# A spare product behind every product of the key loops of a graph network kernel, and seven PSUM banks instead of eight

## The chip, the cores and the metric

The kernel is one program on 1 core of a Trainium2 chip. The metric is the device time of one execution in microseconds (us). The engines are TensorE (PE, with its weight loads shown as PEld), VectorE (DVE), ScalarE (ACT), GpSimd (POOL) and SyncE (SP); 16 DMA engines move the data.

## The reference

Four graph networks run one after the other on 3125 nodes and 50000 edges, each followed by a residual sum and a layer norm. The first one is a two-layer attention network, and the change lies in its scores:

```python
for l in range(L):                                  # two layers
    xn = _layernorm(h, ln1_g[l], ln1_b[l])
    q = (xn @ wq[l] + bq[l]).reshape(n, H, DH)      # 8 heads of 32: 256 numbers a node
    k = (xn @ wk[l] + bk[l]).reshape(n, H, DH)
    v = (xn @ wv[l] + bv[l]).reshape(n, H, DH)
    scores = jnp.einsum('ehd,ehd->eh', q[dst], k[src]) * scale
    m = jax.ops.segment_max(scores, dst, num_segments=n)
    ex = jnp.exp(scores - m[dst])
    z = jax.ops.segment_sum(ex, dst, num_segments=n)
    agg = segment_sum((ex / z[dst])[:, :, None] * v[src], dst)
    ...
```

All data are float32. `dst` is sorted, so the edges of 128 successive rows have their targets in few nodes.

## The kernel before

The edges are laid out in T = 416 tiles of 128, and G = 104 groups of four tiles. For each of the two layers there is a key loop (the names are `k0` and `k1`) over the 104 groups, which makes the scores, and later a value loop (`v0`, `v1`), which sums the weighted values. The third and fourth network have edge loops of their own (`l1`, `l3`), which gather rows in the same manner. The stages follow each other: the scan after a key loop needs all its scores.

Each engine runs its own instruction stream in order, and semaphores tie them. In group i of a key loop:

- POOL issues four indirect DMAs (L944), each of which gathers 128 rows of 512 numbers (key and value of the edge's source) into a ring of five groups. Before group i it waits until group i-5 is scored, and until the value half of that slot has been written out.
- SP loads the places of the targets (LOCT), and DVE makes a one-hot matrix of them (L1466), three groups ahead. ACT copies the window of queries that belongs to each tile into QS (L2082), also three groups ahead.
- PE multiplies the one-hot by the queries (L2517), one product of 264 columns for each tile: the query of each edge, and 8 more columns. Products go round the eight PSUM banks, so that product n waits until product n-8 has been used (the semaphore `self_edge`). Each second product gives an increment of `q_edge`. A float32 product stands in the profile as two MATMUL records and two LDWEIGHTS records.
- DVE multiplies the gathered keys by the bank (L1485, one for each tile; before the first and the third of a group it waits on `q_edge`), then sums by head (L1488). This last one is what POOL waits for, as `scored`.
- ACT takes the last 8 columns of the bank after DVE's multiplication (L2093), and so frees the bank. It also issues the write of the value half to DRAM (L2090, queue q10).

The one-hot of group i+3 stands in DVE's stream behind the sum of group i, and in layer 0 a small step of another job (L1451 to L1457) stands behind that.

Of the kernel before, what the change touches and what calls it, by code (L numbers as in the profile page):

```python
# [17 lines left out]
T = 416  # L18
# [112 lines left out]
def program(nc, a, out):  # L131
    V, S, P, GP, SY = nc.vector, nc.scalar, nc.tensor, nc.gpsimd, nc.sync
# [14 lines left out]
    def view(o, *dims):  # L147
        n = int(np.prod(dims))
        ap = arena[:, o:o + n]
        if len(dims) == 1:  # L150
            return ap
        names = "abcd"[:len(dims)]
        return ap.rearrange("p (%s) -> p %s" % (" ".join(names), " ".join(names)),
                            **{names[i]: dims[i] for i in range(len(dims))})
# [10 lines left out]
    o_misc = take(4 * T + 1288)  # L165
# [17 lines left out]
    def misc(*dims, dt=F):  # L183
        ap = view(mo[0], *dims)
        mo[0] += int(np.prod(dims))
        assert mo[0] <= o_misc + 4 * T + 1288
        return ap if dt == F else ap.bitcast(dt)

    wd_i, ws_i, isrc, idst = (misc(T, dt=I) for _ in range(4))
    ident, iota, ones, tri, sh_1, sh_b = (misc(128) for _ in range(6))  # L190
    g1, a_bc, pcol = (misc(1) for _ in range(3))
    locd = misc(T)
    flag = misc(1, dt=I)
    B = view(o_B, L + 1)
    SC = view(o_S, T, 16)
# [10 lines left out]
    bank = [nc.alloc_psum_tensor(f"bank{i}", [128, 512], F) for i in range(8)]  # L206
# [241 lines left out]
    self_edge = Signal(nc, "self_edge", k0=T, k1=T)  # L448
# [561 lines left out]
    def vector_engine():  # L1010
# [448 lines left out]
        for l in LAYERS:  # L1459
            name = f"k{l}"  # L1460
# [18 lines left out]
            for i in range(G):  # L1479
                rows = KV[:, i % 5, :, 0:256]  # L1480
                V.wait_ge(*gathered(name, i))
                for k in range(4):
                    if k % 2 == 0:
                        V.wait_ge(*q_edge(name, 2 * i + k // 2 + 1))
                    V.tensor_tensor(rows[:, k, :], rows[:, k, :], bank[(4 * i + k) % 8][:, 0:256],  # L1485
                                    ALU.mult).then_inc(qk.sem, 1)
                V.wait_ge(*qk(name, 4 * i + 4))
                V.tensor_reduce(SC[:, 4 * i:4 * i + 4, 0:8], rows.rearrange("p k (h d) -> p k h d", d=32), AX,  # L1488
                                ALU.add).then_inc(scored.sem, 1)
                if i + 3 < G:  # L1490
                    k_onehot(i + 3)
                if l == 0:
                    source_place(i)
                    if i == 12:
                        d.mark(V.tensor_reduce(anyf, B[:, 0:L], AX, ALU.min))
                    elif i == 14:
                        V.wait_ge(*back_in("flags", 1))
                        d.settle()
                        V.tensor_reduce(anyb, B[:, 1:L + 1], AX, ALU.min).then_inc(small_in.sem, 1)

            wn, name = f"w{l}", f"v{l}"
# [27 lines left out]
            for it in range(G + 2):  # L1529
# [4 lines left out]
                if it < G:  # L1534
                    V.wait_ge(*group_in(f"v{l}", it))
                    rows = VR[:, it % VRING].rearrange("p k (h d) -> p k h d", d=32)
                    if it < 2:
                        d.mark(V.memset(WV4[it][:, :, 272:273], 1.0))
                for half in range(2):
                    if it >= 2:  # L1540
                        add_v(name, it - 2, half, v_banks(l, it - 2))
                    if it < G:
                        k = 2 * half
# [198 lines left out]
        for it in range(G + 4):  # L1742
            i = it - 1
            if 0 <= i < G:
                rows = view(o_ring, 6, 4, 72)[:, i % 6]
# [9 lines left out]
            i = it - 2  # L1755
            if 0 <= i < G:
                rows = view(o_ring, 6, 4, 72)[:, i % 6]
# [12 lines left out]
            i = it - 4  # L1770
# [228 lines left out]
    def scalar_engine():  # L1999
# [70 lines left out]
        for l in LAYERS:  # L2070
            if l == 1:
                S.wait_ge(*w_landed(W_LOADS["layer1"]))
            name = f"k{l}"
# [12 lines left out]
            for i in range(G):  # L2086
                if i + 3 < G:
                    stage(i + 3)
                S.wait_ge(*gathered(name, i))
                S.dma_start(VE[i], KV[:, i % 5, :, 256:512]).then_inc(kept[i % 5].sem, 16)  # L2090
                for k in range(4):
                    S.wait_ge(*qk(name, 4 * i + k + 1))
                    S.activation(SC[:, 4 * i + k, 8:16], bank[(4 * i + k) % 8][:, 256:264],  # L2093
                                 ACT.Identity, bias=FL[:, 4 * i + k:4 * i + k + 1]).then_inc(self_edge.sem, 1)
            for k in range(5):
                S.wait_ge(*kept[k]((l + 1) * len(range(k, G, 5))))
# [9 lines left out]
            name = f"v{l}"  # L2106
# [124 lines left out]
        for it in range(G + 4):  # L2231
            if it < 4 * W:
                copy_blocks(2 * it)
            i = it - 1
# [6 lines left out]
            i = it - 2  # L2241
# [91 lines left out]
    def tensor_engine():  # L2333
# [168 lines left out]
        for l in LAYERS:  # L2502
            if l == 1:
                P.wait_ge(*w_landed(W_LOADS["layer1"]))
            name = f"k{l}"
            P.wait_ge(*self_made(f"qkv{l}", W))
            P.wait_ge(*taken(f"mix{l - 1}", 5 * W) if l else taken("qkv0", 3 * W))
            for i in range(G):
                if l == 0 and i == 0:
                    P.wait_ge(*back_in("flags", 1))  # L2510
                P.wait_ge(*onehot(name, i + 1))
                P.wait_ge(*placed(name, i + 1))
                for k in range(4):
                    b_ = bank[(4 * i + k) % 8]
                    if 4 * i + k >= 8:
                        P.wait_ge(*self_edge(name, 4 * i + k - 7))
                    mm = P.matmul(b_[:, 0:264], OHQ[:, i % 3, k * 128:(k + 1) * 128], QS[:, i % 4, k, :],  # L2517
                                  start=True, stop=True)
                    if k % 2:
                        mm.then_inc(q_edge.sem, 1)  # L2520
            if l == 0:
                P.wait_ge(*scan_in("w0", 1))
                answer()
                P.transpose(bank[6][0:1, 0:128], anyf, ident)
                P.transpose(bank[6][0:1, 128:256], anyb, ident).then_inc(small_out.sem, 1)
# [326 lines left out]
```

## Time and profile before

| | |
|---|---|
| Median of 3 runs | 5205.84 us (5201.02 to 5213.5) |
| The profiled execution: its time | 5207.07 us |
| The profiled execution: its span | 5205.9 us |
| Mean granted TensorE clock | 0.835 of full speed |
| PE busy | 3587.0 us, 69% of the span |
| DVE busy | 2874.2 us, 55% |
| ACT busy | 1846.5 us, 35% |
| POOL busy | 3690.2 us, 71% |

The span runs from the first to the last instruction. Busy time is the union of an engine's instructions; time in which an engine waits on a semaphore isn't busy. In the tables by stretch, PEclk is the granted clock of TensorE, where 1.00 is 2.4 GHz and 0.50 is 1.2 GHz. A row of the timeline ends with the time that the engine sat idle before it, and what ended the idle time as far as the profile can infer it; "remote" and "issue" mean that it can't name an instruction.

### The profile page before, as it was taken

The page shows a single profiled execution, that of the slowest core. Times are in us where ns is not written, and L with a number is a line of the kernel's source. Part 1 is how long each engine was busy: PE and PEld are TensorE (multiplying, and loading weights), DVE is VectorE, ACT ScalarE, POOL GpSimd, SP SyncE. Part 2 cuts the span into 40 slices and gives each one's busy share as a digit, 9 for nine tenths or more (in the row PEclk, how much of TensorE's full clock was granted, in tenths as well). Part 3 has the DMA queues.
Part 4 walks back from the last instruction along what each step waited for, and adds up shares of the span by engine and source line. Part 5 has one row for each costly group of instructions (what it writes and reads, how often), then busy time and mean ns, then how long its engine had stood idle before and what let it go on. Part 6 is the DMA issues. An engine that isn't in the chain of part 4 may idle for free.

```text
span 5205.9 us, 59946 instructions
## 1 busy us (share of the span) xinstructions
PE 3587.0 (69%) x15291; PEld 2665.8 (51%) x15291; DVE 2874.2 (55%) x6726; ACT 1846.5 (35%) x5462; POOL 3690.2 (71%) x3085
## 2 busy tenths in 40 slices
PE   4554444466897444439979946666589999688886
PEld 3433323344575232326646634444368887577776
DVE  6465556888543454568884336677752224244445
ACT  1143333566333343337753311111120100256565
POOL 4466666888888666678888876666787887866664
PEclk9866676899898667669999868777799999789988
DMA  7688888565324888866653245566569899556565
GB/s 262 195 278 285 270 288 245 130 159 130 55 25 110 273 272 284 276 183 177 169 138 34 14 91 171 172 173 175 100 153 269 240 267 253 152 174 175 174 175 141
DMA packets 710880, 951.03 MB, mean 183 GB/s; under 512 B 273285, under 2 KB 482228, under 8 KB 710408
## 3 DMA queue, kind: packets, MB, share of 16 engines
q0 software_dynamic: 298192, 385.84, 31.0%
q1 hardware_dynamic: 204146, 388.26, 23.7%
q10 hardware_dynamic: 208198, 173.03, 10.1%
q8 instruction: 131, 2.15, 0.2%
q14 instruction: 213, 1.74, 0.1%
HBM read 727.03 MB, written 219.80 MB: 182 GB/s over the span
## 4 chain that ended last, share of the span: by engine, by line
PE 28%; issue 24%; DVE 15%; POOL 15%; another core or an unknown queue 9%; DMA 6%; ACT 2%; DVEq 1%; ACTq 1%; POOLq 0%; SPq 0%
PE bank L2677 10%; POOL ATT L981 7%; POOL sc L967 7%; PE bank L2802 6%; PE bank L2799 4%; DVE arena L1485 3%; DMA sc<-arena 2%; PE bank L2382 2%; PE bank L2517 2%; DMA ATT<-arena 2%; DVE arena L1395 2%; DVE arena L1765 2%; PE bank L2658 1%; DVE arena L1466 1%
## 5 line engine op out<-in xcount | busy, mean ns | idle before, releaser
L944 POOL DMA_INDIRECT arena<-KVT,arena x832 | 800.7, 962 | 484.5 <-issue 268.4
L2517 PE MATMUL bank<-arena 128*128 128x264 f32 x1664 | 599.0, 514 | 674.5 <-issue 332.2
L2517 PEld LDWEIGHTS bank<-arena 128*128 128x128 f32 x1664 | 390.9, 251 | 881.9 <-issue 588.3
L997 POOL DMA_INDIRECT arena<-ATTR,arena x416 | 666.8, 1603 | 152.2 <-issue 152.2
L967 POOL DMA_INDIRECT sc<-arena x391 | 641.4, 1640 | 130.4 <-issue 110.9
L981 POOL DMA_INDIRECT ATT<-arena x391 | 643.1, 1645 | 125.6 <-issue 114.0
L1485 DVE TENSOR_TENSOR arena<-arena,bank 128x256 f32<-128x256 f32 x832 | 297.4, 412 | 579.8 <-remote 426.8
L944 POOL DMA_INDIRECT arena<-X1T,arena x416 | 413.2, 993 | 245.9 <-issue 134.9
L944 POOL DMA_INDIRECT arena<-YT,arena x416 | 407.4, 979 | 218.5 <-issue 106.5
L2474 PE MATMUL bank<-arena 128*128 128x273 f32 x1664 | 455.0, 411 | 141.3 <-DVE arena L1544 91.7
L2290 ACT ACTIVATE arena<-arena 128x128 f32<-128x128 f32 x1248 | 374.8, 387 | 275.9 <-DVE arena L1371 160.8
L2658 PE MATMUL bank<-arena 128*128 128x261 f32 x832 | 318.5, 534 | 194.3 <-DVE arena L1395 156.7
L2802 PE MATMUL bank<-arena 128*128 128x128 f32 x2496 | 397.2, 293 | 79.7 <-issue 78.9
L2802 PEld LDWEIGHTS bank<-arena 128*128 128x128 f32 x2496 | 382.1, 207 | 125.6 <-issue 99.5
L2093 ACT ACTIVATE arena<-bank,arena 128x8 f32<-128x8 f32 x832 | 208.6, 265 | 651.7 <-issue 452.2
L2474 PEld LDWEIGHTS bank<-arena 128*128 128x128 f32 x1664 | 294.4, 191 | 261.8 <-DVE arena L1544 128.0
L1383 DVE TENSOR_TENSOR arena<-arena,bank 128x273 f32 x832 | 363.5, 437 | 114.9 <-DVE arena L1383 69.4
L1944 DVE TENSOR_TENSOR arena<-arena,bank 128x256 f32 x416 | 173.3, 417 | 356.6 <-remote 245.0
L2382 PE MATMUL bank<-arena 128*128 128x256 f32 (+1 forms) x1200 | 312.2, 402 | 55.9 <-ACT arena L2037 22.5
L2658 PEld LDWEIGHTS bank<-arena 128*128 128x128 f32 x832 | 186.1, 252 | 296.8 <-DVE arena L1765 159.5
L2082 ACT ACTIVATE arena<-arena 128x264 f32 x832 | 283.5, 411 | 151.3 <-issue 118.1
L2114 ACT ACTIVATE arena<-arena 128x128 f32<-128x128 f32 x832 | 265.7, 390 | 193.1 <-PE bank L2474 153.9
(334 smaller groups left out, 6434.5 us busy)
## 6 DMA issues: line engine op xcount, KB each, us to landing
VE<-arena ACTq DMA_DIRECT2D x208, 512.0 KB
arena<-VE SPq DMA_DIRECT2D x208, 512.0 KB
left<-ATT SPq DMA_DIRECT2D x250, 320.0 KB
left<-AM SPq DMA_DIRECT2D x250, 320.0 KB
ATT<-arena POOLq DMA_DIRECT2D x25, 1600.0 KB, 6.5
arena<-LOCT SPq DMA_DIRECT2D x156, 256.0 KB
arena<-ATT SPq DMA_DIRECT2D x75, 384.0 KB
AM<-arena ACTq DMA_DIRECT2D x75, 384.0 KB
```

What stands on the lines that cost most here:

```text
L944: GP.indirect_dma_start(out=ring[:, i % n, k, :], out_offset=None, in_=table, in_offset=bass.IndirectOffsetOnAxis(ap=idx[:, 4 * i + k:4 * ...
L967: GP.indirect_dma_start(out=tg3[k], out_offset=bass.IndirectOffsetOnAxis(ap=poss[:, c:c + 1], axis=0), in_=code[:, c:c + 2], in_offset=Non ...
L981: GP.indirect_dma_start(out=ATT, out_offset=bass.IndirectOffsetOnAxis(ap=PLACE[:, c:c + 1], axis=0), in_=ones[:, 0:1], in_offset=None, bou ...
L997: GP.indirect_dma_start(out=PA[:, c, 2:6], out_offset=None, in_=ATTR, in_offset=bass.IndirectOffsetOnAxis(ap=PA[:, c, 0:1].bitcast(I), axi ...
L1485: V.tensor_tensor(rows[:, k, :], rows[:, k, :], bank[(4 * i + k) % 8][:, 0:256], ALU.mult).then_inc(qk.sem, 1)
L2290: ins = S.activation(SCALED[i % 4][:, k, c, :], OH3[:, i % 3, 128 * k:128 * (k + 1)], ACT.Copy, scale=PA[:, 4 * i + k, 2 + c:3 + c])
L2382: mm = P.matmul(b_[:, 0:cols], xt[:, k * 128:(k + 1) * 128], wt[:, k, :], start=(k == 0), stop=(k == 1))
L2474: mm = P.matmul(bank[banks[k]][:, 0:r.shape[-1]], oh[:, k * 128:(k + 1) * 128], r, start=True, stop=True)
L2517: mm = P.matmul(b_[:, 0:264], OHQ[:, i % 3, k * 128:(k + 1) * 128], QS[:, i % 4, k, :], start=True, stop=True)
L2658: mm = P.matmul(bank[4 + k][:, 0:261], OH8[:, i % 8, k * 128:(k + 1) * 128], WV4[i % 2][:, k, 0:261], start=True, stop=True)
L2677: mm = P.matmul(sum_bank(n // W, j)[:, :], left[:, 128 * j:128 * (j + 1)], right[:, u, :], start=(u == 0), stop=(u == W - 1))
L2802: mm = P.matmul(s4[:, 0:m + 1:m], by[:, m, :], r8[:, m + 3:8:4 - m], start=False, stop=(m == 3), skip_group_check=True)
```

## The change

In both key loops each product of L2517 is followed by a second matmul on PE: the 128x128 identity times 384 columns of constants, into bank 7. Nothing waits for it, nothing reads it, and it gives no increment. Since bank 7 is taken, the real products go round seven banks: product n now waits for the use of product n-7. DVE and ACT read the bank by the same rule.

```diff
@@ program
     ident, iota, ones, tri, sh_1, sh_b = (misc(128) for _ in range(6))
     g1, a_bc, pcol = (misc(1) for _ in range(3))
+    SPARE_COLS = view(o_misc + 4 * T, 384)
@@ vector_engine
-                    V.tensor_tensor(rows[:, k, :], rows[:, k, :], bank[(4 * i + k) % 8][:, 0:256],
+                    V.tensor_tensor(rows[:, k, :], rows[:, k, :], bank[(4 * i + k) % 7][:, 0:256],
                                     ALU.mult).then_inc(qk.sem, 1)
@@ scalar_engine
-                    S.activation(SC[:, 4 * i + k, 8:16], bank[(4 * i + k) % 8][:, 256:264],
+                    S.activation(SC[:, 4 * i + k, 8:16], bank[(4 * i + k) % 7][:, 256:264],
@@ tensor_engine
                 for k in range(4):
-                    b_ = bank[(4 * i + k) % 8]
-                    if 4 * i + k >= 8:
-                        P.wait_ge(*self_edge(name, 4 * i + k - 7))
+                    b_ = bank[(4 * i + k) % 7]
+                    if 4 * i + k >= 7:
+                        P.wait_ge(*self_edge(name, 4 * i + k - 6))
                     mm = P.matmul(b_[:, 0:264], OHQ[:, i % 3, k * 128:(k + 1) * 128], QS[:, i % 4, k, :],
                                   start=True, stop=True)
                     if k % 2:
                         mm.then_inc(q_edge.sem, 1)
+                    P.matmul(bank[7][:, 0:384], ident, SPARE_COLS, start=True, stop=True)
```

The view of 384 columns begins where `ident` begins: it holds `ident`, `iota` and `ones`.

## Rows read from the trace of the kernel before

**Rows 1.** POOL's gathers, one row of the line for each loop: count, duration, starts.
```profile
L944 POOL DMA_INDIRECT arena<-KVT,arena x416: 940/946/2557, 256.5 to 884.9; - x139
...
L944 POOL DMA_INDIRECT arena<-KVT,arena x416: 940/946/1188, 1657.9 to 2287.3; - x139
...
L944 POOL DMA_INDIRECT arena<-YT,arena x416: 940/946/1471, 4535.4 to 5160.1; - x139
```

**Rows 2.** Windows of k0, k1, l1 and l3: us, busy, PEclk, DMA share, GB/s.
```profile
core 0: us, PE busy (x) PEld busy (x) DVE busy (x) ACT busy (x) POOL busy (x), PEclk, DMA share, GB/s
275.00:899.00 624.00, 300.99 (x831) 197.90 (x832) 371.90 (x727) 242.95 (x822) 393.98 (x405) 0.69 0.84 278
1665.00:2295.00 630.00, 290.50 (x816) 187.93 (x816) 309.62 (x616) 232.84 (x812) 394.75 (x415) 0.69 0.83 275
3057.00:3757.00 700.00, 447.04 (x1873) 308.98 (x1873) 462.04 (x1351) 117.92 (x409) 447.43 (x439) 0.77 0.58 158
4535.00:5163.00 628.00, 524.75 (x3229) 474.96 (x3230) 276.80 (x605) 369.42 (x1231) 407.56 (x417) 0.90 0.61 174
```

**Rows 3.** One turn of POOL's cycle in k0, windows of its gathers alone.
```profile
535.98:566.82 30.84, 23.47 (x24) 0.72 0.93 317
566.82:572.47 5.65, 0.00 (x1) 0.50 0.26 82
```

**Rows 4.** POOL's waits in the stretch of k0: us in total, times, longest.
```profile
POOL arena L944 <- issue: 127.6, 379, 2.5
POOL arena L944 <- DVE arena L1488: 87.5, 18, 6.6
POOL arena L944 <- DMA VE<-arena: 4.7, 6, 3.2
```

**Rows 5.** Timeline of PE in that turn: start, us, what, count [idle before].
```profile
534.48 2.13 PE L2517 MATMUL bank<-arena 128*128 128x264 f32 x4 [0.58 <-ACT arena L2093]
537.74 6.14 PE L2517 MATMUL bank<-arena 128*128 128x264 f32 x16 [1.13 <-ACT arena L2093]
544.75 2.02 PE L2517 MATMUL bank<-arena 128*128 128x264 f32 x8 [0.86 <-ACT arena L2082]
548.31 2.02 PE L2517 MATMUL bank<-arena 128*128 128x264 f32 x8 [1.54 <-issue]
551.82 1.13 PE L2517 MATMUL bank<-arena 128*128 128x264 f32 x4 [1.49 <-issue]
556.17 2.13 PE L2517 MATMUL bank<-arena 128*128 128x264 f32 x4 [3.22 <-issue]
566.91 2.10 PE L2517 MATMUL bank<-arena 128*128 128x264 f32 x4 [8.61 <-issue]
```

**Rows 6.** Timeline of DVE in that turn, and one wait of the next.
```profile
547.13 1.40 DVE L1485 TENSOR_TENSOR arena<-arena,bank 128x256 f32<-128x256 f32 x4
...
550.98 0.73 DVE L1485 TENSOR_TENSOR arena<-arena,bank 128x256 f32<-128x256 f32 x2
555.39 0.75 DVE L1485 TENSOR_TENSOR arena<-arena,bank 128x256 f32<-128x256 f32 x2 [3.69 <-remote]
...
566.04 0.75 DVE L1485 TENSOR_TENSOR arena<-arena,bank 128x256 f32<-128x256 f32 x2 [7.71 <-remote]
570.19 0.75 DVE L1485 TENSOR_TENSOR arena<-arena,bank 128x256 f32<-128x256 f32 x2 [3.40 <-PE bank L2517]
570.98 1.22 DVE L1488 TENSOR_REDUCE arena<-arena 128x32 f32<-128x1024 f32 x1
...
591.12 0.75 DVE L1485 TENSOR_TENSOR arena<-arena,bank 128x256 f32<-128x256 f32 x2 [3.19 <-issue]
```

**Rows 7.** Records since the loop began: first PE (L2517), then DVE (L1485).
```profile
270.00:554.00 284.00, 142.73 (x388) 93.89 (x388) 0.68 0.84 284
...
270.00:554.00 284.00, 66.44 (x186) 0.68 0.84 284
```

**Rows 8.** Windows inside that turn, all engines.
```profile
533.50:542.40 8.90, 7.18 (x16) 4.68 (x16) 8.59 (x17) 5.40 (x18) 4.89 (x6) 0.50 0.56 165
542.60:551.70 9.10, 5.33 (x22) 3.64 (x20) 9.03 (x19) 6.06 (x21) 6.92 (x7) 1.00 1.02 346
...
569.60:572.40 2.80, 1.43 (x3) 1.18 (x4) 2.17 (x4) 1.37 (x5) 0.00 (x0) 0.50 0.00 0
```

**Rows 9.** PE in l3, timeline of one stretch.
```profile
4742.95 0.83 PE L2802 MATMUL bank<-arena 128*128 128x128 f32 x6
4743.62 0.60 PE L2799 MATMUL bank<-arena 128*128 128x256 f32 x2
4744.05 0.83 PE L2802 MATMUL bank<-arena 128*128 128x128 f32 x6
```

**Rows 10.** POOL's waits in l3.
```profile
POOL arena L944 <- issue: 106.5, 347, 0.5
POOL arena L944 <- remote: 83.9, 49, 3.8
POOL arena L944 <- PE bank L2802: 28.1, 20, 1.8
```

## The prediction

> **What bounds the kernel now.** The page gives no engine above 71% of the span, so the share of busy time decides nothing; I read the change's own loops. First the gathers by line: POOL issues 416 of them from 256.5 to 884.9 in k0 and from 1657.9 to 2287.3 in k1 [rows 1]. That is 628.4/415 = 1.514 us each, 6.06 us a group, and 6.07 in k1. Then the windows: in both key loops PE is busy for less than half the time at a mean clock of 0.69, DVE for 60% and 49%, and the DMA engines for 0.84 and 0.83 [rows 2]. Nothing is full. So I looked at one turn of POOL's pattern. It issues 24 gathers, six groups, in 30.84 us, 5.14 a group, and then stands still for 5.65 us [rows 3]; 36.49/6 = 6.08 us a group, which is the rate of the whole loop. Its waits for DVE's head sum are 87.5 us in 18 such places [rows 4].
>
> What holds DVE at the end of a turn? It waits 3.69 us before 555.39, 7.71 before 566.04 and 3.40 before 570.19 [rows 6]. The counts say what these are: by 554.0 PE has 388 records since the loop began, which are 194 products, and DVE has started 186 multiplications [rows 7]. Products 187 and 188, for which DVE waits until 555.39, stand in PE's row that ends at 546.77 (544.75 + 2.02) [rows 5]. The wait is the one on `q_edge` (the wait on the gather stands before the first tile of the group, and this is its third). So an increment of PE comes 8.6 us behind the recorded end of its product. Three more come at once later: DVE goes on at 570.19, when the DMA share has just gone to 0.00 [rows 8], and not again held until the next turn. I call this a hold. What makes it the trace doesn't show. It does show that PE works behind the held product (548.31 and 551.82 [rows 5]) without freeing it; that it sets in while the clock is 1.00 and the DMA share 1.02 [rows 8]; and when: POOL starts its run at 535.98 and DVE's first held step ends 19.4 us later; it starts again at 572.47 and that step ends at 591.12, 18.7 us later [rows 3, 6]. It looks tied to POOL's run, not to what PE does.
>
> The key loops are thus bound by a chain: hold, head sum, five slots of the ring, POOL. PE has slack, and between holds DVE sets the pace: 547.13 to 550.98 is 3.85 us for a group [rows 6].
>
> **The change part by part.** *Spare products:* 832 of them. Four real products take 2.02 us at clock 1.00, the last one's own duration included [rows 5]; by starts I use the edge loop l3, which has the same operation and nothing between: 256 columns take 4744.05 - 4743.62 = 0.43 us, three times 128 columns 0.67 [rows 9]. That is 0.0017 us a column: 264 columns take 0.445 us and 384 take 0.65. At clock 0.50 four records of a row (two products) take 2.13 us against 1.13 [rows 5], so everything doubles. A product with its spare is 1.09 us at 1.00, 2.18 at 0.50; a group is 4.4 or 8.7 us, against 1.8 or 3.6 before. The weight loads of 0.19 us lie beside the columns. *Work added:* 832 x 0.65 = 541 us at full clock. If all of it lay on the path, the time would be 5747; but 4.4 us is under POOL's 5.14 a group, so none of it must. That cover is gone while the clock is 0.50 (8.7 over 5.14).
>
> *Seven banks:* PE can run 7 products ahead of ACT and not 8. In the row at 551.82 it is at its limit [rows 5], so it stops one product sooner during a hold. It then has nothing to deliver that isn't held, and at the end of a hold the increments that DVE needs are of products long done. I cost this at 0 to 0.1 us a turn; with 35 turns at most 4 us. *Addressing on DVE and ACT:* nothing. *Queues:* in PE's stream the spare stands between the first product of a pair and the second, which alone increments: each increment is 0.65 us later at full clock, 1.3 at half. Behind it wait DVE's multiplication, ACT's L2093 and, through the head sum, POOL. SP and POOL issue nothing new.
>
> *What this does to a turn.* From 534.48 to 546.77 PE makes 14 products (4, 16 and 8 records [rows 5]). With spares, and the clock at 0.50 until 542.5 as now [rows 8], it makes (542.5 - 534.5)/2.18 = 3.7, then 4.3/1.09 = 3.9: 7.6 products, 6.4 fewer. If the denser work raises the clock 3 us sooner, it is 9.0, 5 fewer. That is 1.25 to 1.6 groups fewer before the hold sets in, if it sets in at the same time after POOL's start. DVE has then scored fewer groups, POOL's run ends as many groups sooner (ring of five), and the stop of 5.65 us stays. A turn of n groups takes 5.14n + 5.65: n = 6 gives 6.08 a group, 4.75 gives 6.33, 4.4 gives 6.42. Over 208 groups that is +52 to +71 us; I take +60. The bounds: PE's lead of 8 products at the start of a turn hides all, 0; a whole two groups are lost, 6.55, +98.
>
> *Sum:* the profiled span is 5205.9 us with 1.2 us around it, 5207.1, and the median of the runs is 5205.8, so one stands for the other. 5206 + 60 = **5266 us**.
>
> At one place a page of the Trainium skill bears on the step of the hold. Perfetto Trace Analysis, section Tensor Engine Instruction, says that the profiler's end of a matmul is an estimate and that its semaphore goes out once PSUM has acknowledged all bytes. The 8.6 us above is such a gap, if the page is right; by it a spare product, which writes 384 more columns, could be one more thing to acknowledge and lengthen a hold, and no row before has one.
>
> **The rivals.**
>
> *No change.* PE's 4.4 us stay under POOL's 5.14, and the lead of 8 products covers the cold start. For it: l3 is as dense as the changed loops would be (PE busy 524.75 of 628, clock 0.90 [rows 2]) and POOL gets 624.7/415 = 1.505 us a gather, 6.02 a group [rows 1], the same. Against: l3 has a lower DMA load, 174 against 278 GB/s [rows 2], and its stops are short, at most 3.8 us [rows 10] against 6.6. Time: 5206, within 10 us.
>
> *Faster: the holds shrink.* In l3 with its dense PE the longest wait of POOL is 3.8 us, and POOL's waits but for the regular 0.3 us are 112 us, against 92 in k0 [rows 4, 10]. If PE that is never idle, or stays at 1.00, gets its increments out sooner, stops go. With no stop at all POOL's 5.14 would hold: 208 x 0.94 = 196 us, 5010. If half of the stops goes: 5108. The point from which this decides is a stop under 5.65 us with six groups still in a turn. Against it: PE's work behind the held product frees nothing now [rows 5], and l3's total is no smaller.
>
> *Slower by much: the half clock.* If the clock stays at its mean of 0.69, a product with spare takes 1.09/0.69 = 1.58 us, 37.9 us for the 24 of a turn, and PE idles some 10 us of it in the holds as now (8.61 and 3.22 [rows 5]): 48/6 = 8.0 us a group, +400 us, 5606. For it: the idle stretches before 556.17 and 566.91 are what the clock falls in now, 0.50 by 569.6 [rows 8]. Against: l3 has 0.90, l1 0.77 with PE busy 64% [rows 2]; the changed loops need PE for 4.4 of some 6.3 us, 70%. The Trainium skill, TensorE: Matmul & The Clock Gate, section What's actually happening, says that the throttled state is the default and activity releases it, which the rows of l3 bear out.
>
> *The change doesn't do its work* can't be: the spare is an instruction like the others and depends on nothing.
>
> **How the numbers follow.** Fewer groups a turn, +20 to +110: 0.42. No change: 0.15. Holds shrink: 0.28, half of it below 5110. Half clock, wholly or for a good part: 0.09. Longer holds as by the page, +110 to +200: 0.06. What a measurement here can tell from no change is 0.2%, 10 us. Slower: 0.42 + 0.09 + 0.06 = 0.57; same 0.15; faster 0.28. The range of 8 in 10 reaches from 5115 (the holds half gone) to 5345 (+98 and some of the longer holds); the likeliest case alone has 5226 to 5316.
>
> **What would show it.** In the profile after: a row of PE with 832 records a loop for the spare, starts 1.09 us apart at 1.00; PE busy in the key loops from 49% to some 75%, clock above 0.8; POOL's turns of 4 or 5 groups with stops near 5.65 us, and its starts in k0 655 rather than 628 us apart. Stops of 2 to 3 us with six groups would show the faster rival; PE in one unbroken row at 0.50 that ends last before DVE, the half clock. I am wrong if the hold isn't tied to POOL's run but to PE's idleness or to the number of products behind it: then the sign turns.

## The result, and the profile after

The changed kernel takes 5252.19 us (median of 4 runs, 5246.43 to 5258.68) against 5203.43 us for the kernel before (4 runs, 5196.83 to 5213.5). The ratio is 1.0095, interval 1.0081 to 1.011: 49 us slower, where 60 were forecast. The profiled execution took 5248.5 us, its span is 5247.4, which is 41.5 above that of before, and the mean granted clock rose from 0.835 to 0.885. Lines of the changed kernel stand one further down: L945 is L944 of before, L1486, L1489, L2094 and L2518 are L1485, L1488, L2093 and L2517, and the spare is L2522.

The first view is that of [rows 1], the gathers of each loop; the three answers and the row of `l1` are put together here.

```profile
L945 POOL DMA_INDIRECT arena<-KVT,arena x416: 940/946/2552, 260.7 to 909.0; - x139
...
L945 POOL DMA_INDIRECT arena<-KVT,arena x416: 940/946/1207, 1677.9 to 2325.6; - x139
...
L945 POOL DMA_INDIRECT arena<-YT,arena x416: 940/946/1439, 4577.6 to 5199.0; - x139
```

From the first gather to the last, `k0` went from 628.4 to 648.3 us and `k1` from 629.4 to 647.7: 6.25 and 6.24 us a group against 6.06 and 6.07. These 38.2 us are nearly all of the 41.5. `l3`, which the change doesn't touch, is the same but for 3.3 us (621.4 against 624.7), and the first gather starts 4.2 us later.

The windows of the same loops, as in [rows 2], say what filled them:

```profile
core 0: us, PE busy (x) PEld busy (x) DVE busy (x) ACT busy (x) POOL busy (x), PEclk, DMA share, GB/s
275.00:919.00 644.00, 505.95 (x1653) 333.63 (x1654) 374.12 (x729) 248.39 (x826) 400.06 (x408) 0.90 0.84 271
1686.00:2335.00 649.00, 504.84 (x1630) 333.30 (x1629) 307.85 (x610) 232.46 (x807) 394.26 (x414) 0.88 0.82 268
4577.00:5205.00 628.00, 524.68 (x3233) 475.51 (x3234) 276.69 (x605) 370.29 (x1234) 408.30 (x417) 0.90 0.63 175
```

PE is busy for 78 to 79% of both key loops at a clock of 0.90 and 0.88, where it was busy for 46 to 48% at 0.69, and is still not full.

POOL's waits in `k0` answer to [rows 4]:

```profile
POOL arena L945 <- issue: 138.6, 384, 2.9
POOL arena L945 <- DVE arena L1489: 99.6, 26, 5.8
...
POOL arena L945 <- DMA VE<-arena: 1.5, 5, 0.3
```

There are 26 waits for the head sum instead of 18, and they are shorter: 3.8 us on the mean against 4.9. POOL's timeline shows the new turn, of which the first and the last gathers stand here (the column in brackets is POOL's idle time before the row):

```profile
496.18 0.94 POOL L945 DMA_INDIRECT arena<-KVT,arena  x1 [4.54 <-DVE arena L1489]
497.43 0.95 POOL L945 DMA_INDIRECT arena<-KVT,arena  x1 [0.30 <-issue]
...
515.24 0.95 POOL L945 DMA_INDIRECT arena<-KVT,arena  x1 [0.30 <-issue]
521.28 0.94 POOL L945 DMA_INDIRECT arena<-KVT,arena  x1 [5.09 <-DVE arena L1489]
...
546.48 0.94 POOL L945 DMA_INDIRECT arena<-KVT,arena  x1 [4.34 <-DVE arena L1489]
```

From 496.18 to 515.24 POOL starts 16 gathers, four groups where [rows 3] had six, and stands still for 5.09 us. The turn is 521.28 - 496.18 = 25.10 us, 6.28 a group.

Now the chain inside that turn. First DVE, as in [rows 6]:

```profile
500.35 1.39 DVE L1486 TENSOR_TENSOR arena<-arena,bank 128x256 f32<-128x256 f32 x4
...
503.83 1.40 DVE L1486 TENSOR_TENSOR arena<-arena,bank 128x256 f32<-128x256 f32 x4
505.27 1.22 DVE L1489 TENSOR_REDUCE arena<-arena 128x32 f32<-128x1024 f32 x1
...
509.19 0.75 DVE L1486 TENSOR_TENSOR arena<-arena,bank 128x256 f32<-128x256 f32 x2 [1.76 <-PE bank L2518]
519.00 0.75 DVE L1486 TENSOR_TENSOR arena<-arena,bank 128x256 f32<-128x256 f32 x2 [9.06 <-remote]
519.79 1.22 DVE L1489 TENSOR_REDUCE arena<-arena 128x32 f32<-128x1024 f32 x1
```

Then PE, as in [rows 5], where x2 is one product or one spare:

```profile
504.15 0.61 PE L2518 MATMUL bank<-arena 128*128 128x264 f32 x2
504.60 0.81 PE L2522 MATMUL bank<-arena 128*128 128x384 f32 x2
505.24 0.61 PE L2518 MATMUL bank<-arena 128*128 128x264 f32 x2
505.69 0.81 PE L2522 MATMUL bank<-arena 128*128 128x384 f32 x2
506.33 0.61 PE L2518 MATMUL bank<-arena 128*128 128x264 f32 x2
...
511.78 0.61 PE L2518 MATMUL bank<-arena 128*128 128x264 f32 x2
512.23 0.81 PE L2522 MATMUL bank<-arena 128*128 128x384 f32 x2
519.77 1.25 PE L2518 MATMUL bank<-arena 128*128 128x264 f32 x2 [6.74 <-ACT arena L2094]
```

And the counts since the loop began, as in [rows 7], of PE's L2518 and then of DVE's L1486:

```profile
270.00:519.50 249.50, 103.23 (x306) 0.90 0.82 269
...
270.00:518.90 248.90, 52.62 (x146) 0.90 0.82 269
```

PE has made 153 products and DVE has started 146 multiplications. The product at 511.78 is thus number 153, and they follow each other by 1.09 us, as forecast. Number 154 needs the bank of number 147: PE stands at the limit of seven banks. Number 148, for which DVE waits until 519.00, starts at 506.33 and ends at 506.94: its increment arrives 12.1 us later, when POOL has been still since 516.19 (515.24 + 0.95). Number 146 ends at 504.76, and DVE, idle for 1.76 us, goes on only at 509.19, 4.4 us behind it. That step is the first of its group and so waits for the gathered rows too, but it isn't these that it waits for: ACT, which waits for the same rows before it issues the write of the value half, issues it at 507.19.

So this hold begins with a product that ends 8.6 us after POOL's start. In the turn of before the first held product ended at 546.77, 10.8 us after POOL's start at 535.98 [rows 3, 5], and two held steps still came through while POOL was issuing, at 555.39 and 566.04 [rows 6]; here it is one, at 509.19. The increments of before weren't the less late: products 189 to 192 stand in the row that ends at 550.33 (548.31 + 2.02) [rows 5], and DVE got the last of them at 570.19, 19.9 us later, when POOL stood still there too. Note also what DVE does until 507: its steps at 500.35 and 503.83 come 3.5 us apart with no idle time before them. PE had products ready. Two turns don't make a rule, though; all turns of the two loops stand below, with the sizes of the spare.

### The profile page after: what moved, and what is told of

Its sections match the earlier page's. It is cut to its first block, busy times and chain, and to the rows that moved or that the text cites. A ratio compares the mean times of both kernels' runs of the same rounds, so it can differ in the third digit from the quotient of the medians.

```text
span 5247.4 us, 63274 instructions
## 1 busy us (share of the span) xinstructions
PE 4020.3 (77%) x16955; PEld 2955.4 (56%) x16955; DVE 2879.2 (55%) x6726; ACT 1852.7 (35%) x5462; POOL 3691.2 (70%) x3085
## 4 chain that ended last, share of the span: by engine, by line
POOL 25%; issue 24%; PE 20%; DVE 11%; another core or an unknown queue 9%; DMA 6%; SPq 3%; DVEq 1%; ACT 1%; POOLq 0%; ACTq 0%
POOL arena L998 12%; POOL sc L968 7%; POOL ATT L982 6%; PE bank L2804 6%; PE bank L2522 5%; PE bank L2518 4%; PE bank L2801 4%; DMA ATT<-arena 3%; DMA sc<-arena 3%; SPq L646 2%; DVE arena L1486 2%; DVE arena L1396 2%; DVE arena L1766 2%; DVE arena L1372 1%
## 5 line engine op out<-in xcount | busy, mean ns | idle before, releaser
L945 POOL DMA_INDIRECT arena<-KVT,arena x832 | 803.8, 966 | 525.5 <-issue 272.3
L2518 PE MATMUL bank<-arena 128*128 128x264 f32 x1664 | 565.5, 424 | 293.5 <-ACT arena L2094 177.9
L2522 PE MATMUL bank<-arena 128*128 128x384 f32 x1664 | 724.4, 519 | 0.0
L2518 PEld LDWEIGHTS bank<-arena 128*128 128x128 f32 x1664 | 334.1, 207 | 574.6 <-ACT arena L2094 227.5
L1486 DVE TENSOR_TENSOR arena<-arena,bank 128x256 f32<-128x256 f32 x832 | 300.3, 414 | 610.7 <-remote 443.5
L945 POOL DMA_INDIRECT arena<-X1T,arena x416 | 412.4, 991 | 247.2 <-issue 136.3
L945 POOL DMA_INDIRECT arena<-YT,arena x416 | 408.0, 981 | 214.6 <-issue 107.1
L2291 ACT ACTIVATE arena<-arena 128x128 f32<-128x128 f32 x1248 | 374.8, 387 | 282.6 <-issue 144.7
L2094 ACT ACTIVATE arena<-bank,arena 128x8 f32<-128x8 f32 x832 | 212.7, 265 | 692.4 <-issue 425.5
L2804 PEld LDWEIGHTS bank<-arena 128*128 128x128 f32 x2496 | 382.3, 206 | 125.1 <-issue 98.5
L2475 PEld LDWEIGHTS bank<-arena 128*128 128x128 f32 x1664 | 295.3, 192 | 263.7 <-DVE arena L1545 136.1
L2522 PEld LDWEIGHTS bank<-arena 128*128 128x128 f32 x1664 | 342.8, 206 | 67.9
L2660 PEld LDWEIGHTS bank<-arena 128*128 128x128 f32 x832 | 188.9, 255 | 283.7 <-DVE arena L1766 138.7
```

The lines of the kernel that those rows point to most:

```text
L945: GP.indirect_dma_start(out=ring[:, i % n, k, :], out_offset=None, in_=table, in_offset=bass.IndirectOffsetOnAxis(ap=idx[:, 4 * i + k:4 * ...
L2291: ins = S.activation(SCALED[i % 4][:, k, c, :], OH3[:, i % 3, 128 * k:128 * (k + 1)], ACT.Copy, scale=PA[:, 4 * i + k, 2 + c:3 + c])
L2475: mm = P.matmul(bank[banks[k]][:, 0:r.shape[-1]], oh[:, k * 128:(k + 1) * 128], r, start=True, stop=True)
L2522: P.matmul(bank[7][:, 0:384], ident, SPARE_COLS, start=True, stop=True)
L2660: mm = P.matmul(bank[4 + k][:, 0:261], OH8[:, i % 8, k * 128:(k + 1) * 128], WV4[i % 2][:, k, 0:261], start=True, stop=True)
L2804: mm = P.matmul(s4[:, 0:m + 1:m], by[:, m, :], r8[:, m + 3:8:4 - m], start=False, stop=(m == 3), skip_group_check=True)
```

## The experiments

The theories at the start were these. *Rate*: PE's time for the spares cuts the number of products made before the hold (the prediction). *Lost bank*: seven banks instead of eight. *Count*: not the time but the number of instructions that PE issues while POOL gathers brings the hold on. *Position*: the increment of each pair stands behind the spare of its first product. In the expectations these are A (*rate*), B (*lost bank*), D and F (*count*) and E (*position*); G, which comes up later, has any matmul behind a product cost the whole, however many records it has. The diffs are against the changed kernel, but for those of `one_pass` and `ring_of_four`, which are against the kernel before.

### The bank alone

`seven_banks` has no spares and keeps the rule of seven.

```diff
-                    P.matmul(bank[7][:, 0:384], ident, SPARE_COLS, start=True, stop=True)
```

> The changed kernel without its spare products: only the seven banks are left. Theory A (PE with its spares makes fewer products before the hold sets in, so POOL's turn has four or five groups instead of six): no change to the kernel before, ratio 0.999 to 1.001, POOL's turns still of 24 gathers, 628 us from first to last gather in k0. Rival B (the lost bank does it: PE stops one product sooner and the hold bites sooner): ratio 1.007 to 1.010, turns of 16 to 20 gathers.

5211.01 us against 5208.06 on the same chip, ratio 1.0004 (0.9993 to 1.0015). *Lost bank* falls: alone it costs nothing that can be told from nothing, as the prediction had it (4 us at most). No run has the spares with eight banks.

### The size of the spare

`spare64` writes 64 columns, `spare512` writes 512.

```diff
-                    P.matmul(bank[7][:, 0:384], ident, SPARE_COLS, start=True, stop=True)
+                    P.matmul(bank[7][:, 0:64], ident, SPARE_COLS[:, 0:64], start=True, stop=True)
```

> The changed kernel with spares of 64 columns instead of 384: a product with its spare takes about 0.56 us at full clock and 1.1 at half. Theory A: in the 12.3 us between POOL's start and the hold PE makes (8/1.1) + (4.3/0.56) = 15 products, no fewer than the 14 of before, so nothing is lost: ratio 0.998 to 1.002, turns of 24 gathers. Rival D (it is the number of instructions or of PSUM writes behind the products that lengthens the hold, not PE's time): ratio 1.006 to 1.010 as in the changed kernel.

> The changed kernel with spares of 512 columns: a product with its spare takes 1.31 us at full clock, 5.25 us a group, above the 5.14 that POOL needs. Theory A: (8/2.6) + (4.3/1.31) = 6.3 products instead of 14 before the hold, 1.9 groups fewer: 6.5 to 6.7 us a group, +90 to +130 us on the kernel before, ratio 1.017 to 1.025. If instead the lead of eight products hides PE's time until it passes POOL's rate: some 1.012.

| spare | us | ratio (interval) | k0, first to last gather |
|---|---|---|---|
| none | 5211.01 | 1.0004 (0.9993 to 1.0015) | 632.5 |
| 64 columns | 5253.84 | 1.0091 (1.0074 to 1.0108) | 649.2 |
| 384 columns | 5252.19 | 1.0095 (1.0081 to 1.011) | 648.3 |
| 512 columns | 5257.04 | 1.01 (1.008 to 1.0119) | 651.7 |

The kernel before took 5208.06 us beside the first, second and fourth, and 5203.43 beside the third. The window 275 to 875 us of the three kernels, in the order none, 64, 512:

```profile
275.00:875.00 600.00, 283.96 (x799) 183.66 (x797) 349.74 (x681) 235.68 (x790) 389.13 (x396) 0.69 0.84 281
```

```profile
275.00:875.00 600.00, 365.56 (x1557) 308.72 (x1558) 345.75 (x673) 235.04 (x779) 373.40 (x384) 0.72 0.82 272
```

```profile
275.00:875.00 600.00, 527.28 (x1525) 297.20 (x1526) 342.48 (x666) 233.23 (x770) 369.20 (x382) 0.96 0.82 271
```

PE's busy time goes from 284 to 366 to 527 us and its clock from 0.69 to 0.72 to 0.96. POOL's gathers in the window, the count beside its busy time, go from 396 to 384 to 382. The whole price comes with the first 64 columns. This is a clear fall of *rate*, and it also clears the clock: 0.72 and 0.96 cost the same. Two of POOL's stops in `spare64` (starts with the idle time before them):

```profile
532.12 0.94 POOL L945 DMA_INDIRECT arena<-KVT,arena  x1 [3.90 <-DVE arena L1489]
557.36 0.94 POOL L945 DMA_INDIRECT arena<-KVT,arena  x1 [4.84 <-DVE arena L1489]
```

What the sizes share shows when all turns of a loop are read in the traces. A turn is here what POOL issues between two stops of over 1.5 us, from the sixth group on. A product counts as held when DVE stands idle for over 0.8 us and starts its multiplication over 1.5 us after the recorded end, with the gathered rows there for over 1 us by ACT's issue of the value half. Each entry has `k0` and `k1`; the last two columns are medians over the 14 to 27 turns that have a held product.

| kernel | turns | groups a turn | products from POOL's start to the first held one | its end, us after POOL's start |
|---|---|---|---|---|
| before | 22, 24 | 4.5, 4.1 | 13, 13 | 10.8, 9.0 |
| no spares, seven banks | 22, 25 | 4.5, 4.0 | 14, 12 | 12.8, 8.5 |
| 64 columns | 28, 30 | 3.5, 3.3 | 8, 7 | 7.0, 5.7 |
| 384 columns | 30, 30 | 3.3, 3.3 | 8, 8 | 8.7, 8.1 |
| 512 columns | 30, 31 | 3.3, 3.2 | 8, 7 | 10.2, 8.5 |

Without spares the hold begins with the 12th to 14th product, with them with the 7th or 8th, whatever the columns. The time at which it begins grows with the columns, and with 512 it is nearly that of the kernel before (10.2 and 8.5 us against 10.8 and 9.0), at the full price; so it isn't an earlier hold that costs, but one after fewer products. In MATMUL records it is some 24 to 28 without spares and 28 to 32 with them, which fits *count* best.

### The place of the spare

`spares_after_pair` puts both spares of a pair behind its increment.

```diff
                     if k % 2:
                         mm.then_inc(q_edge.sem, 1)
-                    P.matmul(bank[7][:, 0:384], ident, SPARE_COLS, start=True, stop=True)
+                        for _ in range(2):
+                            P.matmul(bank[7][:, 0:384], ident, SPARE_COLS, start=True, stop=True)
```

> The same 832 spares of 384 columns, but both of a pair stand behind the pair's second product, so that the increment of a pair isn't 0.65 us (1.3 at half clock) later for the spare in its middle. PE's work is the same. Theory A (PE's rate decides): as the changed kernel, ratio 1.008 to 1.011. Rival E (the lateness of each increment decides): half of the loss goes, ratio 1.003 to 1.006.

5254.04 us against 5208.06, ratio 1.0091 (1.0075 to 1.0108); `k0` takes 647.8 us from its first gather to its last. The same as the changed kernel: *position* falls. Its turns have 3.2 groups, and the first held product is the 8th. Of the four theories *count* is left, and G beside it.

### Fewer and other instructions, on chips that have no holds

The next four were to bend the count: spares in bfloat16 (one MATMUL record each), one spare of 64 columns a group, the real products in one pass without spares, and a ring of four slots instead of five without spares. `one_pass` makes the one-hot and the queries float32r, so the queries are rounded to that type before the product.

```diff
+    IDENT_BF = ident.bitcast(BF)[:, 0:128]
+    COLS_BF = ident.bitcast(BF)[:, 128:192]
...
+                    P.matmul(bank[7][:, 0:64], IDENT_BF, COLS_BF, start=True, stop=True)
```

> The changed kernel with spares of 64 columns in bfloat16 (on the bits of the identity, whatever they say), which are one MATMUL record and one LDWEIGHTS record each and not two: 12 MATMULs a group instead of 16. The spares of 64 columns cost as much as those of 512, so theory A (PE's time) has fallen. Theory F (the number of MATMUL instructions that PE issues while POOL gathers brings the hold on): the loss goes with the records, half of it, ratio 1.003 to 1.006, turns of five groups. Rival G (any instruction behind the product, once it is there, costs the whole): 1.008 to 1.010.

```diff
-                    P.matmul(bank[7][:, 0:384], ident, SPARE_COLS, start=True, stop=True)
+                P.matmul(bank[7][:, 0:64], ident, SPARE_COLS[:, 0:64], start=True, stop=True)
```

> The changed kernel with one spare of 64 columns behind the fourth product of a group only, float32: 10 MATMULs a group. Theory F: a quarter of the loss, ratio 1.001 to 1.004. Rival G: 1.008 or so, if what matters is that a matmul stands behind an increment and before PE's next wait.

```diff
-    OHQ = view(o_acc, 3, 512)
+    OHQ = exact("ohq", o_acc, 3, 512)
-    QS = view(o_acc + 1536, 4, 4, 264)
+    QS = exact("qs", o_acc + 1536, 4, 1056).rearrange("p a (b c) -> p a b c", b=4)
```

> The kernel before, with its real products of the key loops in float32r (the one-hot and the copied queries are written as float32r), without spares, eight banks. The queries are rounded to that type. The hop products of the same kernel, in float32r, have one MATMUL record each, so a group would have 4 records and not 8. Theory F: longer turns, some seven or eight groups, 5.9 to 6.0 us a group, ratio 0.992 to 0.998. Rival G, and theory A with PE's slack: no change, 0.999 to 1.001.

```diff
+                if i >= 4:
+                    GP.wait_ge(*scored(k_, i - 3))
...
-                    GP.wait_ge(*scored(k_, i - 4))
```

> The kernel before, where POOL waits until group i-4 is scored, not i-5, as if the ring of gathered rows had four slots; nothing else. If the hold is tied to what happens during POOL's run and POOL's stop follows when the ring is full, a turn has five groups: (5.14 x 5 + 5.65)/5 = 6.27 us a group, +43 us, ratio 1.006 to 1.010. If a shorter run has a shorter stop, as the changed kernel has (4.3 against 5 us by the median), less: 1.002 to 1.006. If the stops come from the DMA load, which a smaller ring smooths: no change or faster.

They ran on another chip, on which the kernel before took 4811.96 us:

| | us | ratio (interval) |
|---|---|---|
| spare_bf16 | 4813.46 | 0.9998 (0.9985 to 1.0011) |
| spare64_per_group | 4816.67 | 1.0007 (0.9994 to 1.002) |
| one_pass | 4814.43 | 0.9999 (0.9985 to 1.0012) |
| ring_of_four | 4817.73 | 1.0007 (0.9994 to 1.002) |

Nothing here moves the time, and some 395 us are gone from all, the kernel before included. The four can't decide between the theories, since what they disagree about isn't there. So the changed kernel itself was run again on one more chip, beside the spare in bfloat16:

> The changed kernel itself once more, since the last four kernels ran on a chip on which the kernel before takes 4812 us instead of 5208, POOL hardly ever stops in the key loops (5.15 to 5.19 us a group) and no variant differs. If this run falls on such a chip: with no hold there is nothing for the spares to bring forward, PE's 4.4 us a group stay under POOL's 5.15, ratio 0.998 to 1.002. On a chip with holds: 1.008 to 1.011 as recorded.

> The spares of 64 columns in bfloat16, one MATMUL record each, 12 a group, again. On a chip with holds, theory F (the number of MATMUL instructions brings the hold on) expects half of the loss, 1.003 to 1.006, and rival G (any matmul behind the product costs the whole) 1.008 to 1.010. On a chip without holds both expect no change.

On that chip the kernel before took 4814.12 us, the changed one 4811.29, ratio 0.9992 (0.9983 to 1.0001), and the spare in bfloat16 4815.61, 1.0002 (0.999 to 1.0013). The very kernel that costs 0.95% on one chip costs nothing on another. Its gathers in `k0`:

```profile
L945 POOL DMA_INDIRECT arena<-KVT,arena x416: 942/946/2553, 256.8 to 794.8; - x139
```

POOL's waits in the same loop (total, times, longest):

```profile
POOL arena L945 <- issue: 120.3, 395, 0.3
...
POOL arena L945 <- DVE arena L1489: 1.1, 3, 0.5
```

And a window of all engines, the last numbers being clock, DMA share and GB/s:

```profile
275.00:775.00 500.00, 458.01 (x1590) 307.77 (x1589) 359.01 (x691) 234.40 (x795) 379.97 (x387) 0.97 0.98 332
```

POOL needs 538.0/415 = 1.296 us a gather, 5.19 a group, its 395 steady waits are 0.3 us at the longest, and it waits for the head sum 1.1 us in all: this is the 5.14 of a run without the stop [rows 3]. The DMA engines are at 0.98 and 332 GB/s. DVE, where it idles, now waits for the gathered rows and not for PE:

```profile
507.65 1.41 DVE L1486 TENSOR_TENSOR arena<-arena,bank 128x256 f32<-128x256 f32 x4 [3.04 <-DMA arena<-KVT,arena]
517.67 1.41 DVE L1486 TENSOR_TENSOR arena<-arena,bank 128x256 f32<-128x256 f32 x4 [2.84 <-DMA arena<-KVT,arena]
```

And where only the increments of PE count, at the second pair of a group, no step of DVE that had to wait starts later than 0.1 us after the recorded end of the product, in either loop. In the changed kernel with the hold 33 such steps of `k0` waited, up to 15.3 us behind the end, and in the kernel before 29, up to 24.9 us. Without the hold the spares lie wholly under POOL's 5.19 us a group.

It isn't the key loops alone that gain. From the first gather to the last, `l1` and `l3`, which have no spares, went from 658.4 and 621.4 us to 546.2 and 549.6. The four loops together give 420 of the 434 us of span between the two runs of this kernel.

### Half the instructions, and a spare that fills PE

The last two ran on one more chip, which has the hold; the kernel before took 5171.4 us there. `one_pass_again` is `one_pass`, and `two_big_spares` puts two spares of 512 columns behind each product.

> The real products of the key loops in float32r, one MATMUL record each, no spares, eight banks (the queries are rounded to that type), again. On a chip with holds, theory F expects longer turns and 5.9 to 6.0 us a group, ratio 0.992 to 0.998; rival G and theory A no change. On a chip without holds all expect no change.

```diff
-    SPARE_COLS = view(o_misc + 4 * T, 384)
+    SPARE_COLS = view(o_misc + 4 * T, 512)
...
+                    P.matmul(bank[7][:, 0:512], ident, SPARE_COLS, start=True, stop=True)
+                    P.matmul(bank[7][:, 0:512], ident, SPARE_COLS, start=True, stop=True)
```

> The changed kernel with two spares of 512 columns behind each product: a product with its spares takes 0.445 + 2 x 0.87 = 2.2 us at full clock, 8.7 us a group, well over POOL's 5.15. Where is the cover gone? If PE's pace sets the loop then, 104 x 8.7 = 907 us a loop: some 740 us more than before on a chip without holds, 540 to 600 more on one with holds, whatever the holds do. If the loop took less, a spare would be cheaper than its columns.

`one_pass_again` took 5140.45 us, ratio 0.9935 (0.9919 to 0.995): faster than both kernels. Its gathers in `k0`, then a window of it:

```profile
L944 POOL DMA_INDIRECT arena<-KVT,arena x416: 940/946/2552, 263.5 to 860.6; - x139
```

```profile
275.00:875.00 600.00, 174.70 (x431) 112.79 (x429) 375.54 (x729) 250.17 (x830) 400.64 (x411) 0.50 0.90 291
```

POOL's waits in `k0`:

```profile
POOL arena L944 <- issue: 153.4, 403, 4.6
...
POOL arena L944 <- DMA VE<-arena: 30.3, 8, 5.5
```

And two of the stops in POOL's timeline:

```profile
434.10 0.94 POOL L944 DMA_INDIRECT arena<-KVT,arena  x1 [2.44 <-issue]
444.16 0.94 POOL L944 DMA_INDIRECT arena<-KVT,arena  x1 [5.36 <-DMA VE<-arena]
```

A product has one MATMUL record instead of two, and `k0` takes 597.1 us, 5.76 a group. Stops for the head sum are nearly gone; POOL now waits for the write of the value half, 30.3 us in `k0`. The direction is that of *count*, the size 31 us over 208 groups, 0.15 a group against the kernel before on the same chip.

But the hold of this run isn't the old one with fewer instructions. Around the first of the two stops ACT and PE go like this:

```profile
427.68 0.42 ACT L2082 ACTIVATE qs<-arena 128x264 fp32r x1 [0.98 <-issue]
429.08 0.42 ACT L2082 ACTIVATE qs<-arena 128x264 fp32r x1 [0.98 <-issue]
...
433.45 0.59 PE L2517 MATMUL bank<-qs,ohq 128*128 128x264 f32 x1 [0.82 <-ACT arena L2093]
434.84 0.59 PE L2517 MATMUL bank<-qs,ohq 128*128 128x264 f32 x1 [0.81 <-ACT arena L2093]
```

ACT's four copies of a group, 0.31 us apart at the median in the kernel before, stand 1.4 us apart here, and the register operation between each two of them, which waits for no semaphore and has a median of 0.06 us, takes 0.70 us. PE's products follow at the same pace of 1.4 us, and behind the last of them DVE goes on at 435.46, 0.03 us after its recorded end: its increment isn't late at all. In `k0` 97 of the 312 steps from copy to copy within a group are over 1 us, against 2 in the kernel before, and at the second pair of a group no increment is late any more (0.1 us at most). So the engines are held in another way, and part of the effect may lie there. PE's busy time and clock changed too: 175 us in the window where `seven_banks` had 284, and 0.50 throughout. That fewer instructions of the same kind lengthen a turn, this run can't show.

`two_big_spares` took 5711.96 us, ratio 1.104 (1.1021 to 1.106), +541 us. POOL's timeline at its stops, then the window:

```profile
508.17 0.94 POOL L945 DMA_INDIRECT arena<-KVT,arena  x1 [3.95 <-DVE arena L1489]
516.82 0.94 POOL L945 DMA_INDIRECT arena<-KVT,arena  x1 [3.94 <-DVE arena L1489]
525.46 0.94 POOL L945 DMA_INDIRECT arena<-KVT,arena  x1 [3.96 <-DVE arena L1489]
```

```profile
275.00:875.00 600.00, 596.20 (x1650) 314.30 (x1649) 258.32 (x485) 172.30 (x564) 266.38 (x282) 0.99 0.64 200
```

Here the pattern is another one. POOL stops 3.95 us after each group of four, every 8.65 us, and PE is busy 596 of 600 us at a clock of 0.99. PE is the bound now: by the 0.43 us for 256 columns that the prediction read in `l3`, 4 x (264 + 1024) columns are 8.7 us. Here PE's time does set the loop. With 512 spare columns a product it didn't; between 512 and 1024 nothing ran.

## Why the prediction came out as it did

*Sign and size.* +49 us against a forecast of 60, inside the likeliest case's own range.

*Where the time goes.* As forecast it is in the two key loops, 38.2 of 41.5 us of span; `l3` doesn't change.

*Cost of a product with its spare.* 1.09 us by starts at clock 1.00, as worked out; in `two_big_spares` the same figure for a column gives the turn of 8.65 us, and the loops have 8.50 and 8.41 us a group.

*The turn.* As forecast it has four groups, and the bound is still the chain hold, head sum, ring, POOL. The stop was mis-sized: the sum kept 5.65 us, and in `k0` the waits for the head sum are 99.6 us in 26 places, 3.8 us each. With four groups and the old stop the formula gives 5.14 + 5.65/4 = 6.55; the turn shown has 6.28 and the loop 6.25. Over the whole loop a turn went from 4.5 groups to 3.3 in `k0` and from 4.1 to 3.3 in `k1`: the sum set out from a turn of six groups, which is more than the mean, and its loss of 1.25 to 1.6 is near the 1.2 and 0.8 measured. A turn taken too long and a stop taken too long cancelled for the most part. That the total came so near is luck.

*The step that failed* is the one that says "With spares ... it makes ... 7.6 products, 6.4 fewer", with its condition that the hold "sets in at the same time after POOL's start": that PE's time for the spares costs the products. The number came true, 8 products against 13 at the median of all turns; its reason didn't. By it a spare of 64 columns should have cost next to nothing and one of 512 more than one of 384. Measured are 1.0091, 1.0095 and 1.01, with 8 products in 7.0 us of `k0` for 64 columns and 8 in 10.2 us for 512. In place of the time the runs put the spare instructions as such: 8 MATMUL records a group give 6.00 to 6.10 us (the kernel before and `seven_banks`), 16 give 6.24 to 6.30, whatever their columns and place. `one_pass_again`, with 4, had 5.76 and 5.86, on a chip that was itself some 0.7% faster and with a hold of another form.

*The wrong turn that the prediction named* ("the hold isn't tied to POOL's run but to PE's idleness or to the number of products behind it: then the sign turns") half came true: its start goes with what PE issues, and more of it makes it worse, so the sign stood.

*Seven banks.* PE stands at the limit of seven during the hold, and without spares it costs nothing that can be measured, both as forecast.

*Rivals.* No change is what happens on chips without the hold (0.9992), for a reason the prediction didn't have: there POOL alone bounds the loop. Faster by shrinking holds: stops did shrink, but turns shrank with them, so POOL's waits for the head sum rose from 87.5 to 99.6 us. The half clock didn't come: 0.90. The Trainium skill, Perfetto Trace Analysis, section Tensor Engine Instruction, has the semaphore leave once PSUM has acknowledged all bytes; that fits an end that is recorded early, though no run shows PSUM's acknowledgement; but a spare that writes 8 times the bytes (512 against 64 columns) costs the loop nothing more, so the amount written isn't what the price goes by.

*What stays open.* What makes the hold, and why only some runs have it. Each chip was used at one time only, so the chip and the occasion aren't told apart. Whether MATMULs, weight loads or products count, and whether their number counts at all or any matmul behind a product costs the whole (G): the two kernels that would have told (one spare a group, spares in bfloat16) ran only without the hold, and so did the ring of four.

One rival stands outside all the theories, and the traces speak for it: the recording. The traces hold records of semaphore updates beside those of instructions. Where there is no hold these are complete: in `changed_again` all 416 increments of `q_edge` and all 832 behind DVE's multiplications. With the hold they have gaps: 314 and 301 in the kernel before, 337 and 414 in the changed one. So whatever holds the increments also loses records, and it may be that the writing of the records, one for each instruction, is what the engines wait for. That would explain why the number of instructions matters and not their size, and the pace of ACT's register operations in `one_pass_again`. It isn't shown: no run here is known to be without the recording, and the time lost may then not be lost without it.

## What to carry to other kernels

A matmul that nothing waits for and that fits under the bound of its loop isn't free for that, as the spare of 64 columns shows: price the instruction apart from its columns, by a run with the smallest spare beside one with the largest. Where an engine's increment comes many microseconds after its recorded end, find out first whether it does so on every chip, and whether it does so without the profiler; an edit that cost 1% on one chip here cost nothing on the next. And read all turns of a loop before a cause is taken from one: the two turns shown in detail had their first hold 8.6 and 10.8 us in, but with 512 columns it came nearly as late as without spares, at the same price. Halving the instructions of a product by a one-pass type, where its rounding is allowed, gave 0.65% in the one run that has the hold and nothing without it.

## What the runs showed of the hardware that was not expected

- PE's increments can arrive long after the recorded end of the product: 8.6 and 19.9 us in the turn of before, 4.4 and 12.1 us in that of after, the longer of each only once POOL had stopped its gathers. At the second pairs of `k0` the longest are 24.9 and 15.3 us.
- This goes with the chip or with the occasion. The same kernel before took 5203 us beside the changed kernel, 5208 and 5171 us in the two other sets of runs with the hold, and 4812 and 4814 us on two chips without it. There POOL's gathers ran without stops (the changed kernel 5.19 us a group in `k0`, against 6.25 with the hold). The difference, some 400 us, is eight times what the change costs where it costs most.
- A float32 spare of 64 columns costs the loop as much as one of 512, though PE's busy time in the window differs by 162 us. The hold begins with the 7th or 8th product of a turn with spares of any size, and with the 12th to 14th without (medians).
- With the hold the traces lack semaphore records (314 of 416 increments of `q_edge` in the kernel before), without it they lack none.
